# Inverse products of a chunked delta-rule kernel: from full-array products to 64 by 64 products on quarters of the array

## What is computed

```
q, k, v = silu(short_conv(h @ w))            # q and k are then l2-normed
St = St * exp(g_t)                           # 128 x 128 state, decay per channel
St = St + beta_t * k_t (v_t - k_t St)^T
o_t = q_t St
```

## Time and profile before

| | |
|---|---|
| median of 3 runs | 11357.07 us (11350.77 to 11360.08) |
| the profiled execution's own time | 11355.7 us |
| its span | 11353.9 us |
| PE (matmul) busy | 10689.9 us, 94% |
| PEld (weight load) busy | 8366.8 us, 74% |
| DVE busy | 8372.5 us, 74% |
| ACT busy | 5523.6 us, 49% |
| POOL busy | 3967.6 us, 35% |

### The profile page before, as it was taken

How to read it: one execution, slowest core, us unless ns; L and a number is a source line. 1 busy time by engine, 2 the same in 40 slices (tenths; PEclk the granted TensorE clock), 3 DMA queues, 4 the chain that set the end, 5 groups by cost and what they waited for, 6 DMA issues and landing times. The chain is left out here.

```text
span 11353.9 us, 227194 instructions
## 1 busy us (share of the span) xinstructions
PE 10689.9 (94%) x69092; PEld 8366.8 (74%) x69092; DVE 8372.5 (74%) x15387; ACT 5523.6 (49%) x10908; POOL 3967.6 (35%) x6740
## 2 busy tenths in 40 slices
PE   4999999999999999999999999999999999997888
PEld 1777877787787778777778777777787777785333
DVE  2788878888888878887888878887888878885111
ACT  1555555555555555555555555555555555553211
POOL 0343333343334334333433433433343333331000
PEclk7999999999999999999999999999999999998999
DMA  1111111111111111111111111111111111111000
GB/s 43 30 30 30 31 30 30 29 32 30 29 31 30 30 29 32 30 29 31 30 30 31 31 30 29 32 30 29 29 32 30 29 32 29 30 32 37 11 7 11
DMA packets 512439, 332.39 MB, mean 29 GB/s; under 512 B 63088, under 2 KB 510320, under 8 KB 512384
## 3 DMA queue, kind: packets, MB, share of 16 engines
q1 hardware_dynamic: 511328, 327.85, 10.9%
q0 software_dynamic: 1088, 4.26, 0.1%
HBM read 289.48 MB, written 42.47 MB: 29 GB/s over the span
## 5 line engine op out<-in xcount | busy, mean ns | idle before, releaser
L1098 POOL TENSOR_TENSOR KB<-KB,tot 128x256 f32<-128x256 f32 x1548 | 1127.2, 728 | 3513.2 <-PE bank L587 3513.2
L1174 DVE SCALAR_TENSOR_TENSOR acc<-bank,hp,acc 128x510 f32<-128x510 f32 (+2 forms) x2331 | 1727.0, 741 | 119.0 <-ACT hnew L837 64.0
L587 PEld LDWEIGHTS bank<-QKF,KB 128*128 128x128 f32 x12384 | 1549.7, 191 | 282.9 <-issue 249.1
L856 ACT ACTIVATE invE<-bank 128x256 f32<-128x256 f32 x1288 | 491.3, 381 | 2549.0 <-PE bank L620 2549.0
L606 PEld LDWEIGHTS bank<-invE,BIG 128*128 128x128 f32 x12360 | 1544.5, 192 | 253.3 <-issue 202.5
L552 PE MATMUL bank<-hn,w_qkv 128*128 (+1 forms) x3108 | 1529.0, 615 | 172.6 <-DVE acc L1174 128.3
L587 PE MATMUL bank<-QKF,KB 128*128 128x128 f32 x12384 | 1673.9, 278 | 8.7 <-DVE QKF L1253 3.3
L613 PEld LDWEIGHTS bank<-invT,Zm 128*128 128x128 f32 x12360 | 1524.6, 192 | 122.9 <-issue 122.9
L606 PE MATMUL bank<-invE,BIG 128*128 128x64 f32 x12360 | 1564.2, 270 | 1.3 <-DVE BIG L1235 0.7
L613 PE MATMUL bank<-invT,Zm 128*128 128x64 f32 x12360 | 1549.8, 268 | 0.0
L1235 DVE COPY_PREDICATED BIG<-masks,bank 128x512 f32<-128x512 int32 x1290 | 1223.1, 948 | 260.0 <-PE bank L587 187.0
(11 more groups left out here) (196 smaller groups left out, 18877.1 us busy)
## 6 DMA issues: line engine op xcount, KB each, us to landing
bb<-beta_rows SPq DMA_DIRECT2D x518, 128.0 KB, 4.0
states<-StC SPq DMA_DIRECT2D x288, 128.0 KB, 4.0
w_qkv<-in_L_attn_wq_dram SPq DMA_DIRECT2D x260, 128.0 KB, 2.1
w_qkv<-in_L_attn_wv_dram SPq DMA_DIRECT2D x260, 128.0 KB, 3.5
w_qkv<-in_L_attn_wk_dram SPq DMA_DIRECT2D x260, 128.0 KB, 3.1
StA<-states SPq DMA_DIRECT2D x257, 128.0 KB, 2.1
w_o<-in_L_attn_wo_dram SPq DMA_DIRECT2D x257, 128.0 KB, 2.1
w_fb<-in_L_attn_f_b_dram SPq DMA_DIRECT2D x260, 64.0 KB, 3.2
```

Of the source, the lines that this page charges most:

```text
L587: mm = eng.matmul(ps[:, :, ch, :, :], kb[:, ch, :], QKF[par][:, :, ch, :].rearrange("p f (n two m) -> p f n two m", two=2, m=m)[:, :, :, 1 ...
L1098: eng.tensor_tensor(e_, e_, t_.to_broadcast([P, C, P // (2 * m), m]), ALU.mult).then_inc(ev[f"kb_mul{s}"], 1)
L1174: eng.scalar_tensor_tensor(dst, rows(bk)[:, :, 0:BLK - sh], hp[par][:, w_:w_ + 1], dst, ALU.mult, ALU.add).then_inc(ev[("tap_" if t_ < 2 e ...
```

## The change

`z_product` and `y_product` are rewritten. For levels 1 to 5 each chunk's product becomes two products, one for each 64 x 64 quarter on the diagonal (`h` = 0, 1): weights of 64 rows and 64 columns, 32 columns moving. For level 6 each chunk stays one product, with weights of 64 x 64 and 64 columns moving. The evictions `take_zm` and `grow_inverse` become two instructions of 64 partitions and 128 elements for levels 1 to 5, and one of 64 partitions and 256 elements for level 6. Before each of these products there is one more `sem_inc` on TensorE.

The bank table `BK` is new, and the `step` lists of all five engines are in a new order. Some operations change the step in which they run: z, y and turn of level 3, `level(6)`, `keys_back` and `out_sums` run one step later, at its beginning, `state(1)` too; `project_z`, `take_z`, `clip_z` and `softplus_exp` run one step earlier; `key_start` one later. The loads of SyncE are reordered: `load_w(0)`, `load_wo`, `load_gb` one step later, `load_state` one earlier.

The core of the diff:

```diff
-                        for ch in range(C):
-                            mm = eng.matmul(bank[BK[f"z{s}"]][:, ch * HALF:(ch + 1) * HALF], Am[s][:, ch, :], src[:, ch, :], start=True, stop=True)
+                        eng.sem_inc(waited, 1)
+                        ps = bank[BK[f"z{s}"]]
+                        if s == LEVELS - 1:
+                            for ch in range(C):
+                                mm = eng.matmul(ps[HALF:, ch * HALF:(ch + 1) * HALF], Am[s][0:HALF, ch, HALF:], src[0:HALF, ch, :], start=True, stop=True)
+                        else:
+                            for ch in range(C):
+                                for h in range(2):
+                                    rw = slice(h * HALF, (h + 1) * HALF)
+                                    mm = eng.matmul(ps[rw, ch * HALF + h * QUART:ch * HALF + (h + 1) * QUART], Am[s][rw, ch, rw],
+                                                    src[rw, ch, h * QUART:(h + 1) * QUART], start=True, stop=True)
...
+                            for ch in range(C):
+                                mm = eng.matmul(ps[0:HALF, ch * HALF:(ch + 1) * HALF], Zm[s][HALF:, ch, 0:HALF], invT[par][HALF:, ch, HALF:],
+                                                start=True, stop=True)
...
+                                    mm = eng.matmul(ps[rw, ch * HALF + h * QUART:ch * HALF + (h + 1) * QUART], Zm[s][rw, ch, rw],
+                                                    invT[par][rw, ch, rw].rearrange("p (n two m) -> p n two m", two=2, m=1 << s)[:, :, 1, :],
+                                                    start=True, stop=True)
...
-                        eng.activation(blocks(Zm[s][:, :, :], s)[:, :, :, 0, :],
-                                       bank[BK[f"z{s}"]][:, 0:C * HALF].rearrange("p (c n m) -> p c n m", c=C, m=1 << s),
-                                       ACT.Copy).then_inc(ev[f"z_cp{s}"], 1)
+                            for h in range(2):
+                                rw = slice(h * HALF, (h + 1) * HALF)
+                                x_ = eng.activation(blocks(Zm[s][rw, :, rw], s)[:, :, :, 0, :],
+                                                    ps[rw, :, h * QUART:(h + 1) * QUART].rearrange("p c (n m) -> p c n m", m=1 << s), ACT.Copy)
...
-                        o_ = blocks(invT[par][:, :, :], s)[:, :, :, 1, :]
-                        eng.tensor_tensor(o_, o_, ps, ALU.subtract).then_inc(ev[f"inv_m{s}"], 1)
+                            for h in range(2):
+                                rw = slice(h * HALF, (h + 1) * HALF)
+                                o_ = blocks(invT[par][rw, :, rw], s)[:, :, :, 1, :]
+                                x_ = eng.tensor_tensor(o_, o_, ps[rw, :, h * QUART:(h + 1) * QUART].rearrange("p c (n m) -> p c n m", m=1 << s),
+                                                       ALU.subtract)
```

More of the change, by code:

```diff
@@ L690, in step @@
                         read(eng, "t_cp2", i + 1)
+                        if on(i + 1):
+                            z_product(3, i + 1)
+                        read(eng, "zp_in", i + 3)
                         if on(i + 3):
                             project(1, i + 3)
+                        read(eng, "z_g", i)
+                        if on(i + 1):
+                            y_product(3, i + 1, 1 - par)
+                        read(eng, "R_cp1", i)
+                        if on(i):
+                            state(1, i)
+                        read(eng, "z_cp3", i + 1)
+                        if on(i + 1):
+                            level(6, i + 1, 1 - par)
                         read(eng, "lvl_e5", i + 1)
                         if on(i + 1):
+                            turn(3, i + 1, 1 - par)
+                        read(eng, "lvl_e4", i + 1)
+                        if on(i + 2):
+                            diag(i + 2)
+                        read(eng, "inv_m3", i + 1)
+                        if on(i + 1):
                             z_product(4, i + 1)
[L696 to L699, removed]
+                        read(eng, "lvl_e6", i + 1)
                         if on(i + 2):
@@ L743, in step @@
                             z_product(6, i + 1)
-                        read(eng, "inv_m5", i + 1)
-                        if on(i + 1):
-                            residual(0, i + 1, 1 - par)
+                        read(eng, "z_cp1", i + 2)
+                        if on(i + 4):
+                            project_z(i + 4)
+                        read(eng, "z_cp5", i + 1)
+                        if on(i + 2):
+                            turn(1, i + 2, par)
                         read(eng, "tap2_v", i + 3)
@@ L783, in step @@
                         if on(i + 2):
-                            y_product(2, i + 2, par)
-                        read(eng, "z_cp2", i + 2)
+                            turn(2, i + 2, par)
+                        read(eng, "kss_ln", i + 3)
                         if on(i + 1):
                             outputs(i + 1, 1 - par)
[L788 to L814, removed]
                     def begin_block(o):
@@ L1313, in step @@
                         if on(i + 1):
+                            round_qk(5, i + 1, 1 - par)
+                        if on(i + 2):
+                            round_start(i + 2, par)
+                        if on(i + 1):
+                            grow_inverse(3, i + 1, 1 - par)
+                        if on(i + 3):
+                            conv(1, i + 3, 1 - par)
+                        if on(i):
+                            state_up(1, i, par)
+                        if on(i + 1):
+                            round_keys(6, i + 1)
+                        if on(i + 1):
                             grow_qk(6, i + 1, 1 - par)
                         if on(i + 2):
-                            round_start(i + 2, par)
-                        if on(i + 3):
-                            conv(1, i + 3, 1 - par)
+                            diagonal(i + 2, par)
+                        if on(i + 2):
+                            level_products(0, i + 2, par)
                         if on(i + 2):
@@ L1341, in step @@
                         if on(i + 2):
-                            level_products(1, i + 2, par)
+                            grow_qk(1, i + 2, par)
+                        if on(i + 3):
+                            round_w(i + 3)
+                        if on(i + 2):
+                            round_keys(1, i + 2)
                         if on(i + 2):
                             round_qk(1, i + 2, par)
-                        if on(i):
-                            norm_out(i)
+                        if on(i + 2):
+                            start_inverse_t(i + 2, par)
                         if on(i + 1):
@@ L1396, in step @@
                             round_keys(5, i + 2)
-                        if on(i + 2):
-                            round_qk(5, i + 2, par)
-                        if on(i + 1):
-                            state_up(1, i + 1, 1 - par)
-                        if on(i + 3):
-                            softplus_max(i + 3)
-                        if on(i + 2):
-                            grow_inverse(3, i + 2, par)
-                        if on(i + 2):
-                            round_keys(6, i + 2)
-                        if on(i + 3):
-                            key_hat(i + 3)
                     def end_block(o):
```

308 lines of the change are left out of this document (164 added, 144 removed).

## The result

The changed kernel takes 10986.05 us, median of four runs, against 11358.58: a ratio of 0.9675, 95% interval 0.9658 to 0.9692, 373 us less. The forecast was 10890.

The account below looks back on a forecast made before the run. TensorE was taken to bound the loop at 38.93 us a step; -1.8 us from the products, idle unchanged, gave 37.1, or -465 us over 257 steps: 10890 from 11355.7. Stated range 10700 to 12050.

Parts of the forecast that it names:

- The pace and the load-bound products: TensorE sets the loop's pace; z and y products pay for weight loads, 112 ns each, 57 ns with 64 columns.
- Side by side: Levels 1 to 5: two quarters load and stream together, 0.77 us a product, 0.13 less than 0.895; chance 0.60.
- The rival with quarters one after the other: Levels 1 to 5: quarters don't overlap, 1.23 us a product, +2.8 us a step, about 12000 us; chance 0.27.
- The drain on a change of shape: On TensorE, going into small shapes costs 0.09 + 0.055 us and coming out 0.09 + 0.11, 0.34 for each.
- Level 6 and the neighbours: Two level 6 products take 0.80 us, 0.10 less each; y1 beside z6 drops one way out and in, 0.32 less.
- The `sem_inc`: Extra one on TensorE before each product costs nothing; if it held the array, 2.4 us a step.
- The evictions lie beneath TensorE: Halved evictions add 0.75 us a step on VectorE and 0.9 on ScalarE, covered by TensorE; VectorE 32.2 of some 37.
- The idle time, "unchanged": TensorE's idle time per step about 0.45 + 0.4 where it was 1.05, taken as unchanged, ends 0.3 and 2.1.
- the late load: SyncE's `load_w(0)` goes out 2.9 us after project 1; project 0 waits 0 to 0.8 us, taken as 0.4.
- level 4 and `residual(1)`: Readers behind VectorE and `state_up(0)`: level 4 waits 0.2 to 0.4 us, `residual(1)` another 0.2; 0.45 together.
- The quarters' 1.8 us a step: Sum on TensorE, side by side: 10 x -0.13, 2 x -0.10 and -0.32, giving -1.8 us a step.
- The rival "waits take the gain": VectorE's level chain or project 0's weights hold TensorE, idle 1.05 becomes 2.9; 11357 us, within 100; chance 0.08.

Follow-up runs that it names:

- run 6: Changed kernel with load_w(0) first in SyncE's step, levels 1 to 5 taking all four chunks of one quarter, then of the other: 11040.10 us.
- run 4: Kernel before, old order and whole products, with only the evictions of z and y (ScalarE and VectorE) cut in halves: 11630.09 us.
- run 8: Kernel before, old order and whole products, with only VectorE's evictions of y cut in halves: 11632.08 us.
- run 9: Changed kernel with load_w(0) first in SyncE's step and old 128 by 128 products, evictions still in halves: 10936.34 us.
- run 5: Changed kernel with load_w(0) first in SyncE's step, old 128 by 128 products and whole evictions: 10910.18 us.
- run 1: Changed kernel with one load moved: SyncE issues load_w(0) first in its step instead of behind load_w(1): 10680.55 us.
- run 3: Changed kernel's lists, banks and loads, late load included, with old 128 by 128 products and whole evictions: 11374.51 us.
- run 11: The run 1 kernel with VectorE's grow_inverse 5 moved ahead of start_inverse_t: 10670.11 us.
- run 12: The run 11 kernel with VectorE's round_w also moved, from ahead of round_keys 1 to behind grow_inverse 5: 10605.43 us.
- run 2: Kernel before with quarter products and halved evictions, but the old lists, banks and loads: 11456.98 us.

## Why the prediction was right, and where it was not

**The pace and the load-bound products: right.** Products of 64 moving columns cost their weight load, and 64 columns of weights cost about half, 58 ns from one to the next against 112.

**Side by side: right.** 0.78 us a product against 0.77. The rival with quarters one after the other is out: run 6 shows what same-quarter neighbours cost. One argument for that rival was misread: the loads of before do not wait for each other's end, their records are 192 ns long and start 112 ns apart. Both quarters write one PSUM bank, and in the kernel after their matmuls start 7 ns apart. The rule of the Trainium skill cited for that rival ("TensorEngine Tiling (Array Packing)", Restrictions and Gotchas) does not show here, where the quarters also differ in output partitions. The drain on a change of shape, 0.09 to 0.10 us and an open load, is as in the earlier trace rows.

**Level 6 and the neighbours: right.** y6 is 0.88 us, 0.79 without the wait behind it, and 0.80 was forecast. The pair y1, z6 is 1.06; forecast were 0.77 + 0.80 - 0.32 = 1.25.

**The `sem_inc`: right at nothing.** TensorE stands still for 0.10 us on the way into a product, and 0.09 at the changes of shape in the earlier trace rows, which have no `sem_inc`; no run leaves it out.

**"The evictions lie beneath TensorE": right in the new order, and for the wrong reason.** The term was costed from busy shares (32.2 of 37 us). Runs 4 and 8 show that shares don't cover it: with VectorE at 81%, five times 0.15 us, and what else grew with them, cost 278 us in the old lists. What decides is how far each result stands ahead of its reader: the same halves cost 26 us in the new lists (run 9), so those have the room.

**The idle time, "unchanged": the step that was mis-sized, three times, and not in one direction.** First, the waits of before were taken as 0.9 us that might come back. They were 1.7 by starts, and they did not come back: the new order with the load in time is worth 440 us (run 5). Second, the late load was found at its right place (forecast 2.9 us behind project 1, found 3.0), but sized at 0.4 us a step with 0.8 as its end; it is 1.54. The load takes 4 us and not 2.1 to 3.5 to reach its reader: the earlier trace rows gave 2.1 for wq because it went out alone. In the kernel after it goes out behind the two beta loads and fb (3.9 and 4.0 us to landing on that page) and shows 3.8; in run 1, behind wv alone, 2.2. Third, level 4 and `residual(1)` were to wait 0.45 us; by starts neither waits. The sum had `softplus_max` at 1.74 us, and in the new order it takes 0.68. VectorE's late places are others: level 2, and turns 5, 3, 1 and 4.

**The quarters' 1.8 us a step: right as a cost, and partly eaten by waits.** Take at every place of the step the shortest distance by starts that any run of the same products shows: 36.5 us with whole products, 34.6 with quarters. So without any wait the quarters would save 1.9 a step (an estimate from runs 1, 3, 5, 6, 9, 11, 12 and the kernel after). In the new order with the first load they bring 230 us, 0.9 a step (run 5 to run 1; 256 against the halved evictions of run 9), since waits take 1.4 us of a step in run 1 and 0.3 in run 5. Of the 1.4, 1.2 stand ahead of `level` 2, 3 and 6 and of `turn` 5, 3, 1 and 4, all of which read what VectorE writes. So its chain is probably the next limit; the waits of run 1 name it for `turn` and `level`, and run 12, which changes VectorE's list alone, is 0.25 a step faster than run 11.

So 10890 came within 1% with luck in one term. Along one way through the runs the order gives -440 (run 5), the quarters -230 (run 1), the late load +305 (the kernel after). Along the other the order with its late load gives +23 (run 3) and the quarters -388. Both ways must end at the measured time, to the few us by which the kernel before differs between measurements, since each step is a difference of two runs. What they show is that the parts depend on each other. The forecast had -465 for the quarters and 0 for all waits together. By starts the waits are 2.2 us a step before and 2.5 after. That they came out nearly equal is the luck: 1.7 us of old ones went and 1.7 of the late load came, where the prediction had 0.9 and 0.4.

**The rival "waits take the gain"** had project 0's weights right and the level chain at the wrong level (level 2, not level 4), and happened in part. With the old order it is what happens in full and past zero: run 2 is slower than the kernel before.

## What to carry to other kernels

A product bound by its weight load can be cut into quarters on the diagonal, but count the way in and the way out; at 16 instructions that leaves a gain of 0.12 us of 0.9. When an instruction order is written out by hand, measure the new instructions in the old order, the old in the new, and the queue of transfers by itself: here a gain of 440, a gain of 230 and a loss of 305 us stood in one number, and the gain of the quarters was 388 us or 230 by what stood around them. Read TensorE's waits from the starts of its operations: 1.7 us a step stood behind the 0.9 that showed as idle. An engine at 80% is not a cover; the distance between each of its results and the reader is.

## What the runs showed of the hardware

The same VectorE instruction takes 0.68 us or 1.76 us, and which of the two goes with the GpSimd instruction beside it. `softplus_max` and `start_inverse_t`, both 128 x 512 with all operands in SBUF, kernel before and then after:

```profile
L1197 DVE TENSOR_TENSOR r<-r,zp x259: 678/1752/1765, 304.7 to 10337.4; 128x512 f32<-128x512 f32 x130
...
L1264 DVE TENSOR_TENSOR invT<-ident,BIG x258: 682/685/690, 324.4 to 10323.4; 128x512 f32<-128x512 f32 x129
```

```profile
L1223 DVE TENSOR_TENSOR r<-r,zp x259: 674/677/685, 310.0 to 9956.6; 128x512 f32<-128x512 f32 x130
...
L1290 DVE TENSOR_TENSOR invT<-ident,BIG x258: 676/1759/1776, 336.5 to 9949.1; 128x512 f32<-128x512 f32 x129
...
L1279 DVE TENSOR_SCALAR QKF<-QKF x1804: 406/429/1527, 326.2 to 9962.4; 128x512 f32<-128x512 f32 x181
```

The columns are min, median and max. The order swapped the two: one went from 1.75 to 0.68, the other from 0.69 to 1.76, and `round_qk` has a tail to 1.53 that it did not have (478 ns at most before). GpSimd's `softplus_low`, also a `tensor_tensor` of 128 x 512, before and after:

```profile
L1103 POOL TENSOR_TENSOR u<-u,r x259: 1267/1272/1274, 302.1 to 10333.0; 128x512 f32<-128x512 f32 x130
L1129 POOL TENSOR_TENSOR u<-u,r x259: 1257/1582/2187, 303.1 to 9948.8; 128x512 f32<-128x512 f32 x130
```

The pairing is complete in the traces. In the kernel before, all 257 long `softplus_max` run beside GpSimd's `add_query_squares`, and each ends 0.55 us behind it. In the kernel after, 163 of the 258 `start_inverse_t` are long; each started 0.4 us behind `softplus_low` and ends 0.55 us behind it. 92 have no such neighbour and take 0.68, and in the other 3 it is GpSimd's instruction that is long, 2.19 us. The long `round_qk`, 331 of them, all run beside such an instruction and end 0.28 us behind it. The other way round, in run 12 every `start_inverse_t` starts 0.2 us ahead of `softplus_low`: it takes 0.68 us, and GpSimd's 1.65 where it was 1.27. So these instructions behave as if only one of a pair could run at a time. This is inferred from the pairing; no run took GpSimd's part away. Run 12, which moved the instruction that releases `softplus_low`, took the 1.27 us waits of level 2 with it (71 of 245 steps in run 11, none in run 12).

Of VectorE's 1.6 us more a step in the kernel after, the halves are 0.73. By the groups, `round_qk` takes 1.6 more and `start_inverse_t` 0.7 more, `softplus_max` 1.1 less, and smaller groups less too. It is not the order's price by itself: with whole products VectorE is busy in the same 31.4 us a step in the new order (run 5) as before.
